# A preln graph network with a spectral layer, on one core: the setup of the Sturm sweeps re-divided between VectorE, ScalarE and GpSimd, and a block of ones written by another engine

## The chip, the cores and the metric

The program runs on one core of a Trainium2 chip. The time is the device time of one execution in microseconds (us); lower is better. TensorE (PE) does matrix products, VectorE (DVE), ScalarE (ACT) and GpSimd (POOL) work element by element on 128 partitions, SyncE (SP) issues the transfers. Each engine takes its own instructions in order; between engines, and between an instruction and an earlier one of the same engine whose result it reads, there are semaphores.

## What is computed

```python
h = jnp.maximum(_layernorm(x, axis=-1), 0.0)            # x: 32 x 256 x 128
x = x + _L0_gnn_ref(h, adj, W1, b1, W2, b2)
h = jnp.maximum(_layernorm(x, axis=-1), 0.0)
x = x + _L1_gnn_ref(h, adj, Wg0, bg0, Wg1, bg1, Wih, Whh, bih, bhh)

def _L0_gnn_ref(features, A, W1, b1, W2, b2):
    deg = jnp.sum(A, axis=0) + jnp.sum(A, axis=1) - jnp.diagonal(A)
    d_inv_sqrt = jnp.where(deg > 0, jax.lax.rsqrt(deg), 0.0)
    L_norm = d_inv_sqrt[:, None] * (jnp.diag(deg) - A) * d_inv_sqrt[None, :]
    _, U = jnp.linalg.eigh(L_norm)                       # 256 x 256
    agg = jnp.einsum('mn,bnd->bmd', U.T, features)
    out = jax.nn.relu(agg @ W1 + b1) @ W2 + b2
    return jnp.einsum('nm,bmd->bnd', U, out)
```

`_L1_gnn_ref` is two graph layers followed by four small LSTMs over windows of 1 to 4 rows. The change lies wholly in the eigenvectors of the 256 x 256 matrix.

## The kernel before

The 256 x 256 matrices lie as two blocks of 128 rows side by side on 128 partitions. The program goes through these stages.

First the start: GpSimd fills the constants (`ident`, `below`, `ones`, the zeroed NG, RC and V, `sgn` with ones, the index rows `tau_row` and `tau_col`, L263 to L297), VectorE and TensorE build the normalised Laplacian A with one square root on ScalarE (`sq`, L446) in the middle. ScalarE copies the transposed adjacency `adjT` first (L443).

Then the reduction to tridiagonal form: 255 steps k, one reflector each (VectorE L999 to L1081), every step a chain over VectorE, TensorE, ScalarE and GpSimd. It leaves the off-diagonal elements in NG[:, k, 0], scale factors in RC[:, k, 0:2], inner products in `sh` (ScalarE, L492), and the reflectors in V (GpSimd, L340).

Then the setup of the sweeps (VectorE, L1083 to L1119): the diagonal `dbc` = sh * RC squared, the negated squares `ne2` of the off-diagonal, its absolute values `off`, the Gershgorin bounds (greatest of `gh`, least of `gl`, in bnd[:, 0:2]), their span and its reciprocal bnd[:, 7:8], the first grid point bnd[:, 3:4], and `dbh`, `neh`, `e2mid`, the scaled halves of both diagonals, top half on partitions 0 to 63 and the mirrored bottom half on 64 to 127. `link(ins)` makes the next VectorE instruction wait for ins; `mark(ins)` only counts it. Beside this ScalarE takes the root `sc` of RC (L497), and GpSimd scales V by it to `Vh` (L351, two products), and then adds the gate biases `gate_b` (L368).

Then three sweeps (L1132 on) that count sign changes of a three-term recurrence at 64, 128 and 64 points: VectorE four chained instructions a step (L1165 to L1177), ScalarE the signs into `sgn` (L533), VectorE their changes `chg` (L1127), TensorE the counts (L774). In between, products for the accumulated reflectors are slipped in, with `Vh` as the first input (L647). `sgn` must hold ones in its first column block before the first `changes`. Then come the eigenvectors by a twisted factorisation, some filler products of TensorE ahead of the signs (L820, L823, the latter after the norms z_norm of L1361), U, the layers and the LSTMs.

The order of work on each engine is the order in which it is written.

## Time and profile before

| | |
|---|---|
| median of 3 runs | 1576.59 us (1576.54 to 1576.85) |
| the profiled execution's own time | 1576.68 us |
| its span, first to last instruction | 1574.9 us |
| busy: DVE / PE / ACT / POOL | 1252.9 / 1226.0 / 650.1 / 359.5 us |
| chain that ended last: DVE / PE / issue / ACT | 56 / 32 / 9 / 2 % |
| before the first reflector | 0 to about 18.3 us |
| reduction | to about 761.3 us |
| setup of the sweeps | 761.48 to 771.20 us |
| three sweeps | to about 1034 us |

Times in the trace are us from the span's start, and the profiled execution has some 1.8 us around its span. A row of a timeline is start, length, engine, line, operation, output <- inputs, shapes and count; behind it in brackets how long the engine stood idle before and what it waited for. The time from one start to the next says what an instruction costs its engine; two unchained instructions overlap by a little. Engine names with q are an engine's sequencer.

### The profile page before, as it was taken

How to read it: one execution, taken by the hardware profiler on the slowest of the kernel's cores; microseconds unless marked ns; L12 is line 12 of the kernel's file. 1: busy time of each engine (PE TensorE's matmuls, PEld its weight loads, DVE VectorE, ACT ScalarE, POOL GpSimd, SP SyncE). 2: the span in 40 equal slices, each digit the busy share in tenths (PEclk: the TensorE clock that was granted, in tenths of full speed). 3: DMA queues.
4: the chain of work that ended last, by engine and by line, in shares of the span. 5: the costliest groups of instructions: out<-in, count | busy, mean ns of one | idle time of the engine just before them, and what ended most of it. 6: DMA issues, size and time to landing. Idle time of an engine off the chain costs nothing.

```text
span 1574.9 us, 25121 instructions
## 1 busy us (share of the span) xinstructions
PE 1226.0 (78%) x5747; PEld 1006.4 (64%) x5747; DVE 1252.9 (80%) x6155; ACT 650.1 (41%) x2370; POOL 359.5 (23%) x1884
## 2 busy tenths in 40 slices
PE   6888889999976667777354454374999999999998
PEld 4666677777765555555243333262778789999997
DVE  7999999988888888888999999997682255555555
ACT  2333333443443444322121222250234587968676
POOL 5233323333345555555200000002000001010100
PEclk9999999999999999999967776787999999999999
DMA  7000000000000000000000000000000000001012
GB/s 174 2 1 1 1 1 1 1 1 2 1 1 1 1 1 1 1 1 1 1 0 1 1 0 1 0 1 0 1 1 1 0 1 1 1 1 28 1 28 55
DMA packets 23403, 12.63 MB, mean 8 GB/s; under 512 B 5075, under 2 KB 22230, under 8 KB 23254
## 3 DMA queue, kind: packets, MB, share of 16 engines
q1 hardware_dynamic: 23254, 11.03, 2.9%
q8 instruction: 46, 0.75, 0.2%
q14 instruction: 103, 0.84, 0.2%
HBM read 6.83 MB, written 4.19 MB: 7 GB/s over the span
## 4 chain that ended last, share of the span: by engine, by line
DVE 56%; PE 32%; issue 9%; ACT 2%; DVEq 1%; POOL 0%; POOLq 0%
PE bank L842 8%; DVE A L1081 5%; PE bank L844 5%; PE bank L851 4%; DVE RC L1169 4%; DVE O L1177 3%; DVE junk L1014 3%; DVE zc L1075 3%; DVE wk L1065 3%; DVE pa L1165 3%; DVE pc L1038 3%; DVE O L1173 3%; PE pair L842 2%; DVE gqn L1052 2%; DVE A L1071 2%
## 5 line engine op out<-in xcount | busy, mean ns | idle before, releaser
L490 ACT ACTIVATE ncp<-pc,RC 128x2 f32<-128x2 f32 (+1 forms) x254 | 74.9, 295 | 305.7 <-DVE RC L1041 305.7
L699 PE MATMUL bank<-O,y 128*128 128x2 f32 x510 | 142.3, 349 | 65.3 <-DVE y L1014 59.9
L629 ACT ACTIVATE H<-bank,gate_b 128x128 f32<-128x128 f32 (+2 forms) x468 | 167.4, 467 | 50.8 <-PE bank L844 37.8
L684 PE MATMUL bank<-ident,O 128*128 128x128 f32 x382 | 148.2, 457 | 51.4 <-DVE O L1058 38.1
L699 PEld LDWEIGHTS bank<-O,y 128*128 128x128 f32 x510 | 127.8, 311 | 77.7 <-issue 71.9
L684 PEld LDWEIGHTS bank<-ident,O 128*128 128x128 f32 x382 | 60.1, 197 | 139.4 <-DVE O L1058 139.4
L707 PE MATMUL pair<-ident,pc 128*128 128x128 f32 x381 | 145.2, 450 | 4.4 <-DVE pc L1038 1.1
L842 PE MATMUL bank<-O,WlT 128*128 128x128 f32 (+1 forms) x672 | 144.9, 326 | 4.6 <-DVE O L1445 2.8
L774 PE MATMUL bank<-chg,fold 128*128 128x512 bf16 x64 | 29.9, 594 | 139.2 <-DVE chg L1127 139.2
L319 POOL TENSOR_TENSOR ym<-y,below 128x2 f32<-128x2 f32 (+1 forms) x254 | 49.6, 195 | 349.9 <-DVE y L1024 249.9
L1071 DVE SCALAR_TENSOR_TENSOR A<-pair,cx,A 128x254 f32<-128x254 f32 (+63 forms) x380 | 121.3, 319 | 0.4 <-issue 0.2
L842 PEld LDWEIGHTS bank<-O,WlT 128*128 128x128 f32 x672 | 110.6, 190 | 16.6 <-ACT H L629 8.4
L533 ACT ACTIVATE sgn<-O 128x1024 bf16<-128x1024 f32 (+1 forms) x24 | 32.2, 1341 | 203.4 <-DVE O L1177 203.4
L1081 DVE SCALAR_TENSOR_TENSOR A<-bank,zc,A 128x254 f32<-128x254 f32 (+63 forms) x380 | 111.7, 321 | 4.5
L1470 DVE TENSOR_TENSOR H<-H 128x128 f32<-128x128 f32 (+2 forms) x96 | 33.4, 348 | 91.7 <-ACT H L629 91.7
L774 PEld LDWEIGHTS bank<-chg,fold 128*128 128x128 bf16 x64 | 5.7, 120 | 151.1 <-DVE chg L1127 121.9
L434 POOL COPY Wl<-O 128x344 f32<-128x344 f32 (+1 forms) x24 | 16.9, 753 | 373.0 <-DVE O L1450 373.0
L486 ACT ACTIVATE root<-bank 128x1 f32<-128x1 f32 x255 | 43.7, 171 | 133.6 <-PE bank L690 87.6
L844 PE MATMUL bank<-H,WlT 128*128 128x128 f32 (+1 forms) x480 | 98.2, 286 | 0.0
L695 PE MATMUL pair<-O,A 128*128 128x1 f32 x254 | 74.5, 362 | 24.6 <-DVE A L1081 21.3
L1014 DVE CUSTOM_DVE_ANT_0 junk<-A,bank 128x255 f32<-128x255 f32 (+63 forms) x382 | 89.8, 260 | 0.0
L695 PEld LDWEIGHTS pair<-O,A 128*128 128x128 f32 x254 | 63.7, 311 | 35.4 <-DVE A L1081 32.6
(444 smaller groups left out, 3444.6 us busy)
## 6 DMA issues: line engine op xcount, KB each, us to landing
X<-in_x SPq DMA_DIRECT2D x2, 2048.0 KB, 13.1
out<-X SPq DMA_DIRECT2D x32, 128.0 KB, 1.9
adj_sb<-in_adj SPq DMA_DIRECT2D x1, 256.0 KB, 3.0
W1s<-in_L_gnn_W SPq DMA_DIRECT2D x1, 64.0 KB, 11.1
W2s<-in_L_gnn_W SPq DMA_DIRECT2D x1, 64.0 KB, 4.1
Wg0s<-in_L_gnn_Wg SPq DMA_DIRECT2D x1, 64.0 KB, 3.9
Wg1s<-in_L_gnn_Wg SPq DMA_DIRECT2D x1, 64.0 KB, 3.7
Wl<-in_L_gnn_Wih SPq DMA_DIRECT2D x1, 0.5 KB, 6.9
```

The costliest lines, as they stand in the source:

```text
L490: a(ncp[:, bs], pc[:, bs], ACT.Identity, scale=RC[:, k, 1:2]).then_inc(S["ncp_ready"], 1)
L629: ins = a(gates[:, q, i, 0:n], gate_at(p, q, i), fn, bias=gate_b[:, p - 1, i:i + 1])
L684: ins = nc.tensor.transpose(xb[:, b * P:(b + 1) * P], R[:, b, k, 0:1].to_broadcast([P, P]), idf)
L695: mm(y01, A[:, 1, 0:P], R[:, 1, k, 0:1], start=True, stop=True).then_inc(S["y01_ready"], 1)
L699: ins = mm(sb_[:, 0:2], y[:, 1:2].to_broadcast([P, P]), R[:, 1, k, :], start=True, stop=(k >= P - 1))
L707: nc.tensor.transpose(prow[:, b * P:(b + 1) * P], pc[:, b:b + 1].to_broadcast([P, P]), idf).then_inc(S["prow1_ready" if b else "prow0_read ...
L842: last = mm(gate_at(p, q, i), WlT[:, 0, p - 1, i, :], window(c, p, t, part), start=True, stop=(t == 0))
L844: last = mm(gate_at(p, q, i), WlT[:, 1, p - 1, i, :], hst_at(p, q, n), start=False, stop=True)
L851: last = mm(bank[dst][:, a_ * N:(a_ + 1) * N], H[:, b, 2 * c + a_, :], M[:, b, :], start=(b == 0), stop=(b == 1))
L1014: v.tensor_tensor_reduce(out=junk2[:, b, c0:e], in0=A[:, b, c0:e], in1=xb[:, c0:e], scale=1.0, scalar=0.0, op0=ALU.mult, op1=ALU.add, accu ...
L1071: stt(out=A[:, b, c0 + 1:e], in0=prow[:, c0 + 1:e], scalar=cx[:, b:b + 1], in1=A[:, b, c0 + 1:e], op0=ALU.mult, op1=ALU.add).then_inc(S["a ...
L1081: stt(out=A[:, b, c0 + 1:e], in0=xb[:, c0 + 1:e], scalar=zc[:, b:b + 1], in1=A[:, b, c0 + 1:e], op0=ALU.mult, op1=ALU.add).then_inc(S["upd ...
```

## The change

The block of ones `sgn` (4352 columns in bf16) is no longer written by GpSimd's memset but by a ScalarE copy of a broadcast one, ahead of the copies of `adjT`; the counts of the semaphore `consts` go down by one everywhere. The two squares go to ScalarE, between its last `sh` and the root `sc`. The bounds are made by two VectorE instructions that each combine and take a maximum over the row (the least is the negated greatest of off-sum minus dbc), on one sum `gl` of neighbouring off-values. The copies into `dbh` and `neh` are laid between the one-column steps, and fewer instructions are chained. GpSimd's `Vh` waits for the bounds.

```diff
+            sgn_ones set_ready bounds_ready pre_ready lo_ready uv_ready cut_pre q_ready cut_ab cut_rec cut_g pick_ready cut_wh z_norm z_root z_signed zt_ps zt_cp u_ps u_cp
...
-            for t, val in ((NG, 0.0), (RC, -1.0), (V, 0.0), (sgn, 1.0)):
+            for t, val in ((NG, 0.0), (RC, -1.0), (V, 0.0)):
...
                 act, me = S["wy_act"], S["wy_pool"]
                 if i == 0:
                     pool.wait_ge(act, 1)
+                    pool.wait_ge(S["bounds_ready"], 1)
                     pool.wait_ge(S["v_ready"], K)
                     for b in range(NB):
                         ins = g.tensor_tensor(Vh[:, b], V[:, b], sc[:], ALU.mult)
...
         @block.scalar
         def _(act):
             a = nc.scalar.activation
+            act.wait_ge(S["consts"], 2)
+            a(sgn[:].rearrange("p j c w -> p (j c w)"), ones[:, 0:1].to_broadcast([P, 2 * (CH + 1) * PTS]), ACT.Copy).then_inc(S["sgn_ones"], 1)
             act.wait_ge(S["adjT_rdy"], 1)
             for j in range(NB):
                 a(adjT[:, j].rearrange("p (r b i) -> p b i r", r=2, b=NB), bank[6][:, j * N:(j + 1) * N].rearrange("p (b i r) -> p b i r", b=NB, r=2),
...
                     squares(k + 1)
                 norm1(k)
             act.wait_ge(S["c_ready"], K)
+            a(junk2[:, 0], RC[:, :, 0], ACT.Square).then_inc(S["set_ready"], 1)
+            a(ne2[:, 1:N + 1], NG[:, :, 0], ACT.Square).then_inc(S["set_ready"], 1)
             a(sc[:], RC[:, :, 1], ACT.Sqrt, scale=-1.0).then_inc(S["wy_act"], 1)
 
             def evac(dst, src, scale=1.0):
...
             dve.wait_ge(S["s_hist"], K)
             dve.wait_ge(S["d0_ready"], 1)
             pbs, rnb2 = NG[:, :, 0], junk2[:, 0]
-            v.tensor_copy(dbc[:, 0:1], bank[2][:, 0:1])
-            tt(rnb2, RC[:, :, 0], RC[:, :, 0], ALU.mult)
-            stt(out=ne2[:, 1:N + 1], in0=pbs, scalar=-1.0, in1=pbs, op0=ALU.mult, op1=ALU.mult)
             v.memset(ne2[:, 0:1], 0.0)
+            mark(v.tensor_copy(dbc[:, 0:1], bank[2][:, 0:1]))
             link(stt(out=off[:], in0=pbs, scalar=-1.0, in1=pbs, op0=ALU.mult, op1=ALU.max))
+            mark(v.tensor_copy(gl[:, 0:1], off[:, 0:1]))
+            mark(tt(gl[:, 1:N], off[:, 1:N], off[:, 0:N - 1], ALU.add))
+            dve.wait_ge(S["set_ready"], 1)
             link(tt(dbc[:, 1:N], sh[:, 0:K], rnb2[:, 0:K], ALU.mult))
-            link(ts(ne2[:, 1:N], ne2[:, 1:N], -E2_MIN, None, ALU.min))
-            link(tt(gh[:], dbc[:], off[:], ALU.add))
-            link(tt(gl[:], dbc[:], off[:], ALU.subtract))
-            link(tt(gh[:, 1:N], gh[:, 1:N], off[:, 0:N - 1], ALU.add))
-            link(tt(gl[:, 1:N], gl[:, 1:N], off[:, 0:N - 1], ALU.subtract))
-            link(v.tensor_reduce(bnd[:, 0:1], gh[:], AX.X, ALU.max))
-            link(v.tensor_reduce(bnd[:, 1:2], gl[:], AX.X, ALU.min))
-            link(tt(bnd[:, 2:3], bnd[:, 0:1], bnd[:, 1:2], ALU.subtract))
-            link(ts(bnd[:, 2:3], bnd[:, 2:3], 1e-6, None, ALU.max))
-
-            link(ts(bnd[:, 2:3], bnd[:, 2:3], 1.0 / SPAN, None, ALU.mult))
-            link(v.reciprocal(bnd[:, 7:8], bnd[:, 2:3]))
-            link(ts(bnd[:, 3:4], bnd[:, 1:2], bnd[:, 7:8], -0.005 * SPAN, ALU.mult, ALU.add))
+            v.tensor_tensor_reduce(out=gh[:], in0=dbc[:], in1=gl[:], scale=1.0, scalar=-3.0e38, op0=ALU.add, op1=ALU.max, accum_out=bnd[:, 0:1])
+            (v.tensor_tensor_reduce(out=junk2[:, 1], in0=gl[:], in1=dbc[:], scale=1.0, scalar=-3.0e38, op0=ALU.subtract, op1=ALU.max, accum_out=bnd[:, 5:6]).then_inc(S["bounds_ready"], 1))
+            v.tensor_copy(dbh[0:ROWS], dbc[0:ROWS, 0:STEPS])
+            dve.wait_ge(S["bounds_ready"], 1)
+            ts(bnd[:, 1:2], bnd[:, 5:6], -1.0, None, ALU.mult)
+            mark(tt(bnd[:, 2:3], bnd[:, 0:1], bnd[:, 5:6], ALU.add))
+            dve.wait_ge(S["set_ready"], 2)
+            ts(ne2[:, 1:N], ne2[:, 1:N], -1.0, -E2_MIN, ALU.mult, ALU.min).then_inc(S["dve_link"], 1)
+            n_link[0] += 1
+            dve.wait_ge(S["dve_link"], n_link[0] - 1)
+            mark(ts(bnd[:, 2:3], bnd[:, 2:3], 1e-6, 1.0 / SPAN, ALU.max, ALU.mult))
+            v.tensor_copy(dbh[ROWS:P], dbc[ROWS:P, N - 1:N - 1 - STEPS:-1])
+            dve.wait_ge(S["dve_link"], n_link[0])
+            mark(v.reciprocal(bnd[:, 7:8], bnd[:, 2:3]))
+            v.tensor_copy(neh[0:ROWS], ne2[0:ROWS, 0:STEPS])
+            mark(v.tensor_copy(neh[ROWS:P], ne2[ROWS:P, N:N - STEPS:-1]))
+            dve.wait_ge(S["dve_link"], n_link[0] - 1)
+            mark(ts(bnd[:, 3:4], bnd[:, 1:2], bnd[:, 7:8], -0.005 * SPAN, ALU.mult, ALU.add))
+            dve.wait_ge(S["dve_link"], n_link[0] - 1)
+            ts(dbh[:], dbh[:], bnd[:, 7:8], None, ALU.mult)
+            ts(neh[:], neh[:], bnd[:, 7:8], bnd[:, 7:8], ALU.mult, ALU.mult)
+            ts(e2mid[:], ne2[:, STEPS:STEPS + 1], bnd[:, 7:8], bnd[:, 7:8], ALU.mult, ALU.mult)
             tt(bnd[:, 4:5], bnd[:, 7:8], bnd[:, 7:8], ALU.mult)
             ts(bnd[:, 6:7], bnd[:, 7:8], -1.0, None, ALU.mult)
             step = 1.01 * SPAN / (ROWS * WIDTH[0])
...
             link(stt(out=bnd[:, 5:6], in0=bnd[:, 1:2], scalar=-1.0, in1=bnd[:, 0:1], op0=ALU.mult, op1=ALU.max))
             ts(bnd[:, 5:6], bnd[:, 5:6], bnd[:, 7:8], 8 * 2.0 ** -24, ALU.mult, ALU.mult).then_inc(S["pre_ready"], 1)
 
-            v.tensor_copy(dbh[0:ROWS], dbc[0:ROWS, 0:STEPS])
-            v.tensor_copy(dbh[ROWS:P], dbc[ROWS:P, N - 1:N - 1 - STEPS:-1])
-            v.tensor_copy(neh[0:ROWS], ne2[0:ROWS, 0:STEPS])
-            link(v.tensor_copy(neh[ROWS:P], ne2[ROWS:P, N:N - STEPS:-1]))
-            link(ts(dbh[:], dbh[:], bnd[:, 7:8], None, ALU.mult))
-            link(ts(neh[:], neh[:], bnd[:, 7:8], bnd[:, 7:8], ALU.mult, ALU.mult))
-            link(ts(e2mid[:], ne2[:, STEPS:STEPS + 1], bnd[:, 7:8], bnd[:, 7:8], ALU.mult, ALU.mult))
             def changes(n, w):
+                if n == 0:
+                    dve.wait_ge(S["sgn_ones"], 1)
                 dve.wait_ge(S["sgn_ready"], n + 1)
                 if n % 2 == 0 and n:
                     dve.wait_ge(S["sgn_carry"], n // 2)
```

VectorE at the setup, before, from the last reflector's end on; the names are those of the paragraph on the setup, `junk` holds the squares of RC.

```order
L1087 COPY dbc<-bank 128x1 [waits d0_ready,s_hist,c_ready]
L1088 TENSOR_TENSOR junk<-RC 128x256
L1089 SCALAR_TENSOR_TENSOR ne<-NG 128x256
L1090 MEMSET ne 128x1
L1091 SCALAR_TENSOR_TENSOR off<-NG 128x256
L1092 TENSOR_TENSOR dbc<-sh,junk 128x255 [waits dve_link]
L1093 TENSOR_SCALAR ne<-ne 128x255 [waits dve_link]
L1094 TENSOR_TENSOR gh<-dbc,off 128x256 [waits dve_link]
L1095 TENSOR_TENSOR gl<-dbc,off 128x256 [waits dve_link]
L1096 TENSOR_TENSOR gh<-gh,off 128x255 [waits dve_link]
L1097 TENSOR_TENSOR gl<-gl,off 128x255 [waits dve_link]
L1098 TENSOR_REDUCE bnd<-gh 128x1 [waits dve_link]
```

The same place now. ISA is a VectorE instruction that also accumulates, with a second row for writing the accumulator to `bnd`.

```order
L1092 MEMSET ne 128x1 [waits d0_ready,s_hist,c_ready]
L1093 COPY dbc<-bank 128x1
L1094 SCALAR_TENSOR_TENSOR off<-NG 128x256
L1095 COPY gl<-off 128x1 [waits dve_link]
L1096 TENSOR_TENSOR gl<-off 128x255
L1098 TENSOR_TENSOR dbc<-sh,junk 128x255 [waits set_ready]
L1099 ISA gh,bnd<-dbc,gl 128x256 [waits dve_link]
L1099 ISA bnd 128x1
L1100 ISA junk,bnd<-gl,dbc 128x256
L1100 ISA bnd 128x1
L1101 COPY dbh<-dbc 64x128
L1103 TENSOR_SCALAR bnd<-bnd 128x1 [waits bounds_ready]
```

Two squares are gone from VectorE, one sum stands for four, both reductions are folded into the ISA rows, and a copy of `dbh` stands ahead of the first wait for the bounds.

GpSimd among the constants, before:

```order
L276 MEMSET V 128x512
L276 MEMSET sgn 128x4352
L277 MEMSET eps_col 128x1
L278 IOTA fine 128x32
L280 IOTA junk 128x512
L284 IOTA grid 64x64 [waits consts]
L286 IOTA tau_col 64x4 [waits consts]
L284 IOTA grid 64x64 [waits consts]
```

and now:

```order
L276 MEMSET V 128x512
L277 MEMSET eps_col 128x1
L278 IOTA fine 128x32
L280 IOTA junk 128x512
L284 IOTA grid 64x64 [waits consts]
L286 IOTA tau_col 64x4 [waits consts]
L284 IOTA grid 64x64 [waits consts]
```

The memset of `sgn` is gone, and what stood behind it follows on V.

GpSimd at the end of the reduction, before:

```order
L338 TENSOR_TENSOR vt<-ident,NG 128x1 [waits v_ready,pb_ready,x_ready]
L340 TENSOR_TENSOR V<-O,vt 128x1 [waits vt_ready]
L351 TENSOR_TENSOR Vh<-V,sc 128x256 [waits v_ready,wy_act]
L351 TENSOR_TENSOR Vh<-V,sc 128x256
L368 TENSOR_TENSOR gate_b<-gate_in 128x16 [waits b_in]
L355 AFFINE_SELECT Pm<-Gs 128x512 [waits wy_act]
```

and now:

```order
L338 TENSOR_TENSOR vt<-ident,NG 128x1 [waits v_ready,pb_ready,x_ready]
L340 TENSOR_TENSOR V<-O,vt 128x1 [waits vt_ready]
L352 TENSOR_TENSOR Vh<-V,sc 128x256 [waits v_ready,bounds_ready,wy_act]
L352 TENSOR_TENSOR Vh<-V,sc 128x256
L369 TENSOR_TENSOR gate_b<-gate_in 128x16 [waits b_in]
L356 AFFINE_SELECT Pm<-Gs 128x512 [waits wy_act]
```

The rows are the same; the first product waits for one semaphore more, and the rest stands behind it.

## Rows read from the trace of the kernel before

**Rows 1.** Timeline of the start: start, length, engine, line, operation, operands, count.

```profile
4.69 3.73 POOL L276 MEMSET sgn<- 128x4352 bf16 x1
...
5.03 1.07 ACT L443 ACTIVATE adjT<-pair 128x256 f32<-128x256 f32 x2 [2.96 <-PE pair L662]
...
6.12 1.28 ACT L446 ACT_TABLE_LOAD   x1
...
6.80 1.68 DVE L973 TENSOR_SCALAR pos<-deg 128x2 f32<-128x2 f32 x1
...
9.44 0.20 ACT L446 ACTIVATE sq<-deg 128x2 f32<-128x2 f32 x1 [2.03 <-DVE deg L975]
...
10.07 0.68 DVE L980 TENSOR_SCALAR tmp<-ident,dinv 128x256 f32<-128x256 f32 x2
...
12.11 1.50 POOL L294 TENSOR_SCALAR tau_row<-junk 128x512 bf16<-128x512 f32 x1
...
13.37 0.52 DVE L984 TENSOR_SCALAR tmp<-ident 128x512 f32<-128x512 f32 x1
```

**Rows 2.** Timeline of the setup of the sweeps, up to the first sweep instruction.

```profile
761.48 0.16 DVE L1087 COPY dbc<-bank 128x1 f32<-128x1 f32 x1 [0.23 <-ACT sh L492]
761.56 0.41 DVE L1088 TENSOR_TENSOR junk<-RC 128x256 f32<-128x256 f32 x1
761.79 1.63 POOL L351 TENSOR_TENSOR Vh<-V,sc 128x256 f32<-128x256 f32 x2 [0.40 <-ACT sc L497]
761.89 0.95 DVE L1089 SCALAR_TENSOR_TENSOR ne<-NG 128x256 f32<-128x256 f32 x1
762.77 0.93 DVE L1091 SCALAR_TENSOR_TENSOR off<-NG 128x256 f32<-128x256 f32 x1
...
763.38 0.40 POOL L368 TENSOR_TENSOR gate_b<-gate_in 128x16 f32<-128x16 f32 x1
...
764.52 0.43 DVE L1094 TENSOR_TENSOR gh<-dbc,off 128x256 f32<-128x256 f32 x1
764.98 0.42 DVE L1095 TENSOR_TENSOR gl<-dbc,off 128x256 f32<-128x256 f32 x1
...
768.43 0.15 DVE L1110 SCALAR_TENSOR_TENSOR bnd<-bnd 128x1 f32<-128x1 f32 x1
...
768.74 0.21 DVE L1113 COPY dbh<-dbc 64x128 f32<-64x128 f32 x1
768.96 0.22 DVE L1114 COPY dbh<-dbc 64x128 f32<-64x128 f32 x1
...
770.01 0.35 DVE L1118 TENSOR_SCALAR neh<-neh,bnd 128x128 f32<-128x128 f32 x1
...
770.71 0.25 DVE L1135 TENSOR_SCALAR lam<-grid,bnd 128x64 f32<-128x64 f32 x1
771.20 0.28 DVE L1165 SCALAR_TENSOR_TENSOR pa<-lam,dbh,O 128x64 f32<-128x64 f32 x1 [0.24 <-DVE lam L1135]
```

**Rows 3.** Timeline of the first sweep, where a GpSimd product lies beside VectorE.

```profile
796.51 1.30 POOL L359 TENSOR_TENSOR RT<-ident,PmT 128x512 f32<-128x512 f32 x1 [7.18 <-ACT PmT L500]
796.61 1.28 DVE L1165 SCALAR_TENSOR_TENSOR pa<-lam,dbh,O 128x64 f32<-128x64 f32 x1
```

**Rows 4.** One line's instructions: shortest/median/longest ns, first and last start, forms.

```profile
L533 ACT ACTIVATE sgn<-O x24: 1057/1057/1911, 778.7 to 1027.2; 128x1024 bf16<-128x1024 f32 x16, 128x2048 bf16<-128x2048 f32 x8
```

**Rows 5.** Timeline, VectorE: a product with an accumulated sum.

```profile
1089.54 0.42 DVE L1361 CUSTOM_DVE_ANT_0 junk<-adj_sb 128x256 f32<-128x256 f32 x1
```

**Rows 6.** Timeline of TensorE: its first product with Vh.

```profile
783.77 3.02 PE L647 MATMUL bank<-Vh 128*128 128x256 f32 x8
```

**Rows 7.** Busy by stretch, PE, PEld, DVE, ACT, POOL, then granted clock, DMA, GB/s.

```profile
1084.00:1085.00 1.00, 1.00 (x2) 0.36 (x2) 1.00 (x4) 0.00 (x0) 0.90 (x2) 0.50 0.06 16
```

**Rows 8.** One line's instructions: shortest/median/longest ns, the first filler products.

```profile
L820 PE MATMUL bank<-WlT,ident x10: 592/592/1190, 1083.6 to 1088.9; 128*128 128x512 f32 x10
```

**Rows 9.** Timeline of TensorE: the filler products behind z_norm.

```profile
1090.38 2.84 PE L823 MATMUL bank<-WlT,ident 128*128 128x512 f32 x6 [0.87 <-DVE ssq L1361]
```

15 lines of the change are left out of this document (7 added, 8 removed).

## The prediction

> **What bounds the kernel now.** I read the chain of waits first. It runs through the places that this change touches and nowhere near a DMA: the start up to the first reflector, and a stretch of almost ten microseconds between the reduction and the first sweep in which VectorE works alone. The profiled execution took 1576.68 us against a median of 1576.59, so a sum made in it is moved down by 0.09. The reader needs two timelines.
>
> The start [rows 1]: VectorE's tiny TENSOR_SCALAR on deg (L973, two columns) takes 1.68 us, because it lies beside GpSimd's 3.73 us memset of sgn. It ends only when that memset has ended (4.69 + 3.73 = 8.42). So ScalarE's root sq, ready since its table load ended at 7.40, starts at 9.44, and all that follows hangs on it.
>
> The setup [rows 2]: from L1087 at 761.48 to the first step of the sweep at 771.20 are 9.72 us, nearly all on VectorE and nearly all chained by link. In it, GpSimd's two products Vh (1.63 us together) make two VectorE instructions of 256 columns, L1089 and L1091, take 0.95 and 0.93 us, where L1088 and L1094 of the same width take 0.41 and 0.43. The same is seen in the first sweep [rows 3]: a 64-column instruction lasts 1.28 us beside a GpSimd product of 1.30 us that it began 0.10 us after. So for these kinds of operands one engine stands still until the other's instruction is over; 512 columns hold it about 1.3 us, and 256 columns about 0.66.
>
> **The start, part by part.** The memset leaves GpSimd, so what is behind it moves up 3.7 us. ScalarE instead writes 4352 columns before the two adjT copies. Its row for bf16 from f32 [rows 4] gives 1057 ns for 1024 columns and 1911 for 2048: 0.834 ns a column and 0.20 us fixed, so 3.83 us. Its first table load should end at about 2.1 (the second takes 1.28 us; the first is taken to be as long and to begin at 0.8, an estimate). The write then ends at 5.9; the adjT copies begin about 5.75 in place of 5.03, end at 6.8 (1.07 us), and the table load behind them ends at 8.1 in place of 7.40 [rows 1]. VectorE's three little instructions no longer meet the memset; they meet short copies of GpSimd and should be through by 7.3 to 7.9. So ScalarE's own chain becomes what sq waits for: sq at 8.1, which is 1.3 us early.
>
> That is not kept. L980 follows sq by 0.63 us and would start at 8.75. GpSimd's tau_row, at 12.11 with 1.50 us, moves up to about 8.2 to 8.4 and runs to 9.7 to 9.9. That it holds a TENSOR_SCALAR is in the trace: L984 begins at 13.37 inside it, and ends 0.28 after tau_row's end at 13.61 [rows 1]. So the pair L980 ends at about 10.0 to 10.4, against 10.75 now: 0.35 to 0.75 us gained. L984, no longer beside tau_row, gives another 0.1. I take **0.6 us**; the bounds are 0.1 (the write on ScalarE is slower, or L980 waits for tau_col and fold too) and 1.4 (tau_row does not hold it).
>
> **The setup without GpSimd.** VectorE's new list, start to start [rows 2]: memset and one-column copy 0.16 (L1087 to L1088 is 0.08); off, chained, 0.46 (L1094 to L1095); one-column copy 0.08; gl, which nothing is chained to, 0.33 (L1088 to L1089); dbc, chained, 0.46; the two products with an accumulated maximum. The nearest row for these is the accumulated sum L1361 of 256 columns with 0.42 us [rows 5], and with 0.07 of overlap 0.35 each, 0.70. Together 2.19 us, and both bounds are there at 763.67. A maximum is not in the trace; below this it can hardly go, as 256 columns cost 0.33 at the least in any unchained row, and above it I allow 0.3 us each.
>
> Then, with the copies laid between the one-column steps: copy of dbh until the bounds can be read, 0.13, and two steps of 0.08, 0.29; ne2 0.20; the scaled span, 0.16, since the copy behind it begins at another partition (L1113 to L1114 is 0.22, the whole length of a copy, so such a copy waits for the one before); copy 0.23; reciprocal 0.09; two copies 0.23 and 0.25. That is 1.45. The bnd step 0.13, dbh 0.20 and neh 0.27 (L1135 with 0.25 and L1118 with 0.35, each less 0.08 of overlap, and 0.03 for the wider tile), e2mid 0.20: 0.80. Four last steps: 0.15, and 0.31 as from L1110 to L1113. lam to the first pa, 0.49. The whole is 2.19 + 1.45 + 0.80 + 0.46 + 0.49 = 5.39 us against 9.72: 4.33 us less. What goes is the squares (to ScalarE, which does them right behind the last sh, each 0.42 us by the two lengths in [rows 4], and has them at about 761.7 and 761.9, while VectorE wants them at 762.5 and 764.0), three of the four sums and two reductions, for which one sum and the two accumulating products stand, and most of the chained pauses.
>
> **The wait that is added.** GpSimd's Vh now waits for bounds_ready, about 763.75, and with it gate_b and the rest of GpSimd's queue. TensorE does not mind: its first product with Vh is at 783.77 [rows 6], and Vh would be ready at about 765.3. VectorE does. At 763.8 its next instructions are the two bnd steps and ne2, with two SBUF inputs or of the TENSOR_SCALAR kind, just those that stood still above. Two products of 0.66 us and a small gate_b pass, one VectorE instruction between each: VectorE reaches the scaled span about 1.3 us late, at 765.4 instead of 764.16. So the stall of L1089 and L1091 (1.0 us) is not removed but moved, and it is now 1.3. The setup gains 4.33 - 1.3 = **3.0 us**; first sweep step near 768.2.
>
> Here a page bears on the number. The reported lengths of GpSimd, 1.63 for the pair and 0.40 for gate_b [rows 2], would make the stall 2.0 us. The Trainium skill (Perfetto Trace Analysis, GPSIMD Engine Instruction) says that such spans are unreliable and that instructions are to be timed by start-to-start spacing; the two Vh products end at 763.42 with one VectorE stream of 0.27 us between them, and by that they are 0.68 each. By the reported spans the setup would gain 2.3, by spacing 3.0.
>
> A second page speaks of who is held at all. The Trainium skill (SBUF — State Buffer, Who interferes with whom) says that the pair of ports shared by VectorE and GpSimd is locked for a whole instruction, and that an instruction with two SBUF inputs contends with GpSimd's reads only, one in a two-port mode with anything of GpSimd. L973 beside a memset, and L1165 beside a product, agree with it.
>
> **Sum.** 0.6 + 3.0 = 3.6 us: 1576.68 - 3.6 - 0.09 = **1573.0 us**. The sweeps, the layers and the recurrent part are the same instructions, and only begin earlier.
>
> **Rivals.**
> 1. *No stall in the setup*: the one-column steps pass beside Vh, or VectorE gets ahead. For it: no one-column SBUF step is seen beside a long GpSimd product before. Against: ne2 has 255 columns, and L1091's kind did stand still. Time 1576.59 - 0.6 - 4.3 = 1571.7.
> 2. *tau_row does not hold L980*, if GpSimd's list is later or sooner than I place it. The start gains 1.4: 1576.59 - 1.4 - 3.0 = 1572.2.
> 3. *The stalls are as long as the reported spans, on both places*: 0.4 at the start and 2.3 in the setup, or the accumulated maxima cost 0.3 more each: 1573.9. For it: L973 shows how a tiny instruction can be held through several. Against: the spacing of Vh.
> 4. *Slower*: TensorE's clock. The filler products ahead of the signs, five and then three, begin at granted clock 0.50, the level of 1.2 GHz [rows 7]; each is two records, which go from 1190 to 592 ns when it rises to 2.4 GHz [rows 8]. The last three lie on the chain, 2.84 us for six records, with 0.87 us idle ahead [rows 9]. If the shifted program found the clock low through these six (3.6 us more) and through the two full products behind them (3.0 us more each at most, as much as L647 takes in [rows 6]), it would lose up to 9.6 us and stand at 1582. It costs nothing up to a rise 1.7 us later (0.87 us at half speed), and outweighs the gain of 3.6 from a rise 9 us later. Against: three runs lie within 0.31 us.
>
> **Chances.** Forecast 0.58, rival 1 0.09, rival 2 0.08, rival 3 0.20, rival 4 and other mishaps 0.05. The range from 1571.6 to 1574.2 takes in rivals 1 to 3 and leaves out the fourth and the outer bounds. 0.2% is 3.15 us, about what a measurement can tell from no change, and the line is at 1573.44, near to my number. The forecast lies under it in four of five, rivals 1 and 2 wholly, rival 3 in one of five: 0.69 faster, 0.27 the same, 0.04 slower.
>
> **What would show it.** At the start: sgn on ScalarE of about 3.8 us, L973's counterpart under 0.4 us, sq near 8.1, the pair of tmp at 10.0 to 10.4. In the setup: the maxima at 0.42 us, bnd steps and ne2 of 0.7 to 0.9 us beside Vh, and 6.7 us from the one-column copy to the first pa. Wrong if ScalarE loads a table between the squares and the root, if the bnd steps are short while Vh runs, or if the first pa comes after 769.

## The result and the profile after

The kernel after the change takes 1571.18 us (median of 6 runs, 1570.37 to 1572.52), the kernel before 1576.95 us beside it (6 runs, 1576.54 to 1577.31). The ratio is 0.9966, with a 95% interval of 0.9955 to 0.9976: faster by more than 0.2%, by about 5.8 us where 3.6 were forecast, and 0.4 us below the range of 1571.6 to 1574.2. The profiled execution took 1570.37 us, with a span of 1568.6 us. It is the fastest of the six and lies 0.8 us under their median, where the profile of before lies 0.3 us under its own, so 0.5 us of the distance between the two profiles is spread and not the change.

The page after: the span, the busy times, and the shares of the chain that ended last.

```profile
span 1568.6 us, 25122 instructions
...
PE 1224.6 (78%) x5747; PEld 1005.1 (64%) x5747; DVE 1247.5 (80%) x6153; ACT 657.3 (42%) x2373; POOL 352.9 (22%) x1883
...
DVE 55%; PE 33%; issue 9%; ACT 2%; DVEq 1%; POOL 0%; POOLq 0%
```

VectorE has 5.4 us less work (it had 1252.9). The chain has kept its shares (56 / 32 / 9 / 2 before), so nothing new bounds the kernel. The gain must be looked for by stages. Four marks divide the span: the first `half` (the end of the start), the one-column copy into `dbc` (the end of the reduction), the first `pa`, and the first norm behind the sweeps (z_norm). Each is the start of that VectorE instruction in the timeline.

| us | start | reduction | setup | sweeps | rest |
|---|---|---|---|---|---|
| before | 19.3 | 742.2 | 9.7 | 318.3 | 485.3 |
| before, a second profile | 19.3 | 743.1 | 9.7 | 318.3 | 485.5 |
| after | 18.4 | 741.2 | 6.1 | 317.4 | 485.5 |
| after, a second profile | 18.4 | 742.3 | 6.1 | 318.5 | 485.4 |
| after, a third | 18.4 | 741.0 | 6.1 | 319.0 | 485.2 |

Start and setup repeat to 0.1 us. The reduction and the sweeps differ by up to 1.3 and 1.6 us between executions of one kernel, so of them a single pair of profiles proves nothing.

The start of after, which answers to [rows 1]; columns as there.

```profile
2.08 3.83 ACT L443 ACTIVATE sgn<-ones 128x4352 bf16<-128x4352 f32 x1
...
6.87 1.28 ACT L449 ACT_TABLE_LOAD   x1
...
8.17 0.20 ACT L449 ACTIVATE sq<-deg 128x2 f32<-128x2 f32 x1
8.29 1.50 POOL L294 TENSOR_SCALAR tau_row<-junk 128x512 bf16<-128x512 f32 x1
...
8.61 0.30 DVE L983 TENSOR_TENSOR dinv<-dinv,pos 128x2 f32<-128x2 f32 x1
8.94 0.99 DVE L985 TENSOR_SCALAR tmp<-ident,dinv 128x256 f32<-128x256 f32 x2
...
9.99 2.07 PE L675 MATMUL bank<-tmp,ones 128*128 128x256 f32 x4 [3.56 <-DVE tmp L985]
...
12.55 0.43 DVE L989 TENSOR_SCALAR tmp<-ident 128x512 f32<-128x512 f32 x1
...
18.38 0.16 DVE L1014 TENSOR_SCALAR half<-bank 128x1 f32<-128x1 f32 x1 [0.81 <-PE bank L689]
```

`sgn` on ScalarE is as forecast (2.08, 3.83 us), the root `sq` is at 8.17 instead of 9.44, and `tau_row` lies over the pair of `tmp`, as forecast. But the pair ends at 9.93, under the forecast of 10.0 to 10.4, and the scaled identity (L989, once L984 with 0.52) lasts 0.43. The first `half` comes 0.89 us earlier. The line of the pair, with the shortest, the middle and the longest of the two in ns:

```profile
L985 DVE TENSOR_SCALAR tmp<-ident,dinv x2: 354/538/723, 8.9 to 9.2; 128x256 f32<-128x256 f32 x2
```

The first one passes beside `tau_row` in 0.35 us. The second lasts 0.72 us instead: it is held, and ends 0.14 behind the reported end of `tau_row` (8.29 + 1.50 = 9.79).

The setup of after, which answers to [rows 2].

```profile
759.37 0.42 ACT L500 ACTIVATE junk<-RC 128x256 f32<-128x256 f32 x1
...
759.60 0.16 DVE L1093 COPY dbc<-bank 128x1 f32<-128x1 f32 x1
...
761.33 0.42 DVE L1100 CUSTOM_DVE_ANT_0 junk<-gl,dbc 128x256 f32<-128x256 f32 x1
...
761.81 0.14 DVE L1103 TENSOR_SCALAR bnd<-bnd 128x1 f32<-128x1 f32 x1
761.88 0.14 DVE L1104 TENSOR_TENSOR bnd<-bnd 128x1 f32<-128x1 f32 x1
761.89 1.45 POOL L352 TENSOR_TENSOR Vh<-V,sc 128x256 f32<-128x256 f32 x2 [2.42 <-DVE bnd L1100]
761.94 0.82 DVE L1106 TENSOR_SCALAR ne<-ne 128x255 f32<-128x255 f32 x1
762.68 0.14 DVE L1109 TENSOR_SCALAR bnd<-bnd 128x1 f32<-128x1 f32 x1
762.85 0.57 DVE L1110 COPY dbh<-dbc 64x128 f32<-64x128 f32 x1
763.30 0.21 POOL L369 TENSOR_TENSOR gate_b<-gate_in 128x16 f32<-128x16 f32 x1
...
765.68 0.28 DVE L1175 SCALAR_TENSOR_TENSOR pa<-lam,dbh,O 128x64 f32<-128x64 f32 x1 [0.24 <-DVE lam L1145]
```

From the one-column copy to the first `pa` are 6.08 us (759.60 to 765.68), against 9.72. The squares are on ScalarE, the maxima cost 0.42 us each, like the accumulated sum of [rows 5], and 0.08 for the read of the result. The reader is to see in what order things come at 761.8: both bnd steps (L1103, L1104) are issued before Vh (761.89) and last 0.14. Two VectorE instructions are held, ne2 (0.82) and the copy into `dbh` (0.57). The one-column TENSOR_SCALAR between them, at 762.68 and so in the middle of Vh (its second product is reported from 762.57 to 763.34), lasts 0.14 and is not.

### The profile page after: what moved, and what is told of

Read it like the earlier page. It is cut to its first block, busy times and chain, and to the rows that moved or that the text cites. A ratio compares the mean times of both kernels' runs of the same rounds, so it can differ in the third digit from the quotient of the medians.

```text
span 1568.6 us, 25122 instructions
## 1 busy us (share of the span) xinstructions
PE 1224.6 (78%) x5747; PEld 1005.1 (64%) x5747; DVE 1247.5 (80%) x6153; ACT 657.3 (42%) x2373; POOL 352.9 (22%) x1883
## 4 chain that ended last, share of the span: by engine, by line
DVE 55%; PE 33%; issue 9%; ACT 2%; DVEq 1%; POOL 0%; POOLq 0%
PE bank L847 8%; DVE A L1086 5%; PE bank L849 5%; PE bank L856 4%; DVE RC L1179 4%; DVE O L1187 4%; DVE junk L1019 3%; DVE zc L1080 3%; DVE pc L1043 3%; DVE wk L1070 3%; DVE pa L1175 3%; PE pair L847 3%; DVE O L1183 3%; DVE gqn L1057 2%; DVE A L1076 2%
```

## The experiments

Two questions stood open: how the 5.8 us divide, and what of it is the reduction, whose instructions nobody touched. Times are medians, with the ratio to the kernel before in runs of the same chip and its 95% interval. Five groups of kernels ran, each beside its own runs of before.

### The two kernels again, and each half alone

`before_again` and `after_again` are the two kernels unchanged. `start_only` is before with the change of `sgn` alone:

```diff
-            for t, val in ((NG, 0.0), (RC, -1.0), (V, 0.0), (sgn, 1.0)):
+            for t, val in ((NG, 0.0), (RC, -1.0), (V, 0.0)):
...
+            act.wait_ge(S["consts"], 2)
+            a(sgn[:].rearrange("p j c w -> p (j c w)"), ones[:, 0:1].to_broadcast([P, 2 * (CH + 1) * PTS]), ACT.Copy).then_inc(S["sgn_ones"], 1)
```

`setup_only` is the other half: after with `sgn` still a memset of GpSimd, all else of the change in.

> The kernel before, unchanged, under a second name. Theory A (the two places account for the change, and the rest of the difference between the two profiles, 1.8 us spread over the reduction and what follows the setup, is spread between executions): ratio to before 1.000 within 0.001, and the time from the first reflector's half (L1009) to the one-column copy (L1087) differs from the first profile's 742.2 us by some tenths of a us up to 1 us. Theory B (the change itself makes the reduction and the rest faster): that time repeats within 0.2 us.

> The changed kernel, unchanged, under a second name. Theory A: 4.5 us below before (0.90 at the start, 3.64 in the setup), so ratio 0.9971. Theory B: 5.8 us or more below, ratio 0.9963 or less, and the reduction again about 1 us shorter than in the kernel before.

> The kernel before with the ones of sgn written by ScalarE and nothing else. Theory A: first reflector 0.9 us earlier, as in the profile of the changed kernel, the setup unchanged at 9.72 us; 0.9 us below before, ratio 0.9994. Theory B, that the change at the start also shortens the reduction: 1.9 us or more below. The sum of my prediction had 0.6 us here.

> The changed kernel with sgn written by GpSimd's memset as before, so only the setup is new. Theory A: first reflector where it was before (root at 9.44), setup 6.1 us instead of 9.7, 3.6 us below before, ratio 0.9977. Theory B, a faster rest behind the setup: 4.5 us or more below. The sum of my prediction had 3.0 us here.

| | median us | ratio | start | reduction | setup |
|---|---|---|---|---|---|
| before_again | 1577.24 | 1.0001 [0.9992, 1.0010] | 19.3 | 743.1 | 9.7 |
| after_again | 1571.88 | 0.9969 [0.9958, 0.9981] | 18.4 | 742.3 | 6.1 |
| start_only | 1575.55 | 0.9992 [0.9983, 1.0001] | 18.4 | 742.1 | 9.7 |
| setup_only | 1573.56 | 0.9978 [0.9970, 0.9987] | 19.2 | 742.9 | 6.1 |

The kernel before stood at 1577.18. `setup_only` gains 3.62 us, which is its setup (9.72 - 6.08 = 3.64) and nothing else. `start_only` gains 1.63, of which its start explains 0.9. Together they are 5.25, and `after_again` gains 5.30, between the 4.5 of theory A and the 5.8 of theory B: by the medians the halves add up. The interval of `start_only` reaches 1.0001, so its median can't carry the rest alone; the steps below do. The surplus of 0.7 to 0.8 us belongs to the half that moves `sgn`, but lies behind the first `half`.

To find it I took the distance from each step's first `half` to the next one's. Most of the 254 distances scatter a little. But in steps 3, 19, 35, 51, 67, 83, 99 and 115, sixteen apart, each takes one of two values, 0.05 to 0.18 us from each other: step 83 has 3.37 us in before and 3.26 in after. These eight sum to 28.29 to 28.33 us in `before`, `before_again` and `setup_only`, and to 27.50 to 27.56 in `after`, `after_again` and `start_only`. (Sums of starts read to 0.01 us.) That is 0.8 us, and what was sought. (Behind step 127, steps 187, 188 and 244 differ too, two by -0.1 and one by +0.17, and cancel.)

### What holds VectorE in the setup

`no_bounds_wait` takes out the added wait, so that Vh starts when `sc` is there:

```diff
                     pool.wait_ge(act, 1)
-                    pool.wait_ge(S["bounds_ready"], 1)
                     pool.wait_ge(S["v_ready"], K)
```

`vh_one_column2` keeps the wait and shrinks what waits to one column. It leaves out nearly all of the scaling of V, so its time shows an unhampered setup:

```diff
+            g.memset(Vh[:], 0.0)
...
-                        ins = g.tensor_tensor(Vh[:, b], V[:, b], sc[:], ALU.mult)
+                        ins = g.tensor_tensor(Vh[:, b, 0:1], V[:, b, 0:1], sc[:, 0:1], ALU.mult)
```

> The changed kernel without GpSimd's wait for the bounds: Vh starts when ScalarE's root sc is there, about 0.9 us into the setup. Theory A (a GpSimd product of 256 columns holds each VectorE instruction of two wide SBUF inputs, or of the two-port kind with more than one column, for about 0.66 us wherever it lies): now the dbc product and the first accumulated maximum are held, the setup is about 6.3 us instead of 6.1, 0.2 us slower than the changed kernel, ratio to before 0.9972. Rival (the place does not matter or the wait costs): the setup is 5.2 us, 0.9 us faster than the changed kernel.

> The changed kernel with both products Vh cut to one column each (the rest of Vh is set to zero in the constants, so this leaves out nearly all of the scaling and the eigenvectors aren't computed). Theory A: nothing holds ne2 (0.29 us instead of 0.82) and the second copy of dbh (0.22 instead of 0.57); the setup is 5.2 us instead of 6.1, my sum of unheld durations having been 5.4. Rival (the two are long for another reason, such as the order of partitions): the setup stays at 6.1 us.

`no_bounds_wait`: 1571.32 us, ratio 0.9967 [0.9955, 0.9980], setup 6.1 us. `vh_one_column2`: 1571.34, 0.9967 [0.9954, 0.9979], setup 5.2 us. (Before: 1576.64, for these two and the next two.) The timeline of the setup in `no_bounds_wait`:

```profile
760.75 1.86 POOL L351 TENSOR_TENSOR Vh<-V,sc 128x256 f32<-128x256 f32 x2 [1.05 <-ACT sc L501]
761.20 0.83 DVE L1098 CUSTOM_DVE_ANT_0 gh<-dbc,gl 128x256 f32<-128x256 f32 x1
...
761.96 0.93 DVE L1099 CUSTOM_DVE_ANT_0 junk<-gl,dbc 128x256 f32<-128x256 f32 x1
...
763.10 0.27 DVE L1105 TENSOR_SCALAR ne<-ne 128x255 f32<-128x255 f32 x1
```

Without the wait Vh meets the two maxima instead, which last 0.83 and 0.93 us instead of 0.42, and ne2 is free (0.27). The expectation had named the product into `dbc` and the first maximum; `dbc` starts together with Vh and takes its usual 0.42. The stall is moved, not removed: the setup is 6.13 us against 6.08, so the added wait is worth 0.05 us. The same place in `vh_one_column2`:

```profile
763.17 0.38 POOL L353 TENSOR_TENSOR Vh<-V,sc 128x1 f32<-128x1 f32 x2 [2.42 <-DVE bnd L1101]
763.22 0.28 DVE L1107 TENSOR_SCALAR ne<-ne 128x255 f32<-128x255 f32 x1
763.42 0.14 DVE L1110 TENSOR_SCALAR bnd<-bnd 128x1 f32<-128x1 f32 x1
...
763.59 0.23 DVE L1111 COPY dbh<-dbc 64x128 f32<-64x128 f32 x1
```

Here nothing is held, ne2 takes 0.28 instead of 0.82 and the copy 0.23 instead of 0.57. The two differences are 0.54 + 0.34 = 0.88 us, the same as 6.08 - 5.20 between the setups. So the stall of Vh in after is 0.9 us, and the list without it is 5.2 us.

Yet the kernel with the shorter setup is no faster than after (it gains 5.30 us on its own runs of before, `after_again` on its own as much). Its eight steps sum to 28.37: it has the long ones again, with the change of `sgn` in. It has one more memset of GpSimd in its start, and so had before. That was the first hint.

### Is it the number of GpSimd instructions ahead of the loop?

`after_plus_one` is after with one memset more, a repetition, and `before_minus_one` is before with one memset fewer: of the five memsets of `begin_sweep`, two rows three apart and of one value are written by one.

```diff
+            g.memset(eps_col[:], EPS)
```

```diff
-            begin_sweep()
+            for row, rows, val, d in ((14, 1, 0.0, 1), (15, 1, 1.0, 1), (30, 4, 0.0, 3), (31, 2, 1.0, 1)):
+                ins = g.memset(poly[:, row:row + rows:d], val)
+            ins.then_inc(S["ring_ready"], 1)
```

> The changed kernel with one more GpSimd instruction ahead of the reduction, a memset of the one-column eps_col that repeats its value. Theory C (in every 16th step of the reduction one of GpSimd's instructions comes 0.29 us late, which one depends on how many instructions stand ahead in its stream, and taking the memset of sgn away moved the lateness from ym, for which VectorE waits, to one that nobody waits for): steps 3, 19, 51, 67, 83, 99 and 115 are long again, as in the kernel before (3.37 us for step 83 instead of 3.27), step 244 short again, and the reduction is 0.8 us longer; 0.8 us slower than the changed kernel, ratio to before 0.9974. Rival (ScalarE's writing of sgn, or an earlier start, shortens the steps): step 83 stays at 3.27.

> The kernel before with the first begin_sweep's two zero rows set by one memset instead of two, so one GpSimd instruction fewer ahead of the reduction, nothing else. Theory C: ym is no longer late in every 16th step, step 83 takes 3.27 us instead of 3.37, the reduction is 0.8 us shorter, start and setup as before; ratio 0.9995. Rival: the steps stay as in the kernel before.

`after_plus_one`: 1572.84 us, 0.9972 [0.9961, 0.9983]. `before_minus_one`: 1576.45, 0.9996 [0.9987, 1.0004], with before at 1577.27. Step 83 in four kernels, GpSimd's `ym` and VectorE's `tm`, which reads it. Before:

```profile
309.63 0.20 POOL L319 TENSOR_TENSOR ym<-y,below 128x2 f32<-128x2 f32 x1 [2.15 <-DVE y L1024]
...
309.86 0.22 DVE L1047 SCALAR_TENSOR_TENSOR tm<-ym,RC,tmp 128x2 f32<-128x2 f32 x1 [0.21 <-POOL ym L319]
```

After:

```profile
307.84 0.20 POOL L319 TENSOR_TENSOR ym<-y,below 128x2 f32<-128x2 f32 x1 [1.87 <-DVE y L1029]
...
308.25 0.24 DVE L1052 SCALAR_TENSOR_TENSOR tm<-ym,RC,tmp 128x2 f32<-128x2 f32 x1
```

After plus one memset:

```profile
308.98 0.20 POOL L320 TENSOR_TENSOR ym<-y,below 128x2 f32<-128x2 f32 x1 [2.15 <-DVE y L1030]
...
309.20 0.22 DVE L1053 SCALAR_TENSOR_TENSOR tm<-ym,RC,tmp 128x2 f32<-128x2 f32 x1 [0.20 <-POOL ym L320]
```

Before minus one memset:

```profile
309.06 0.20 POOL L321 TENSOR_TENSOR ym<-y,below 128x2 f32<-128x2 f32 x1 [1.87 <-DVE y L1026]
```

The bracket behind `ym` is GpSimd's idle time: 2.15 us in the first and third, 1.87 in the other two, as in the steps around. In the first and third GpSimd starts `ym` 0.28 us later for no reason that the row names (its input is VectorE's `y` in all four), and `tm` waits for it (0.21 and 0.20 us idle, released by `ym`). All the steps agree: in before and after plus one `ym` starts 0.43 to 0.50 us behind the end of `y` in the eight steps 3, 19, ..., 115 and 0.14 to 0.15 in the rest of the first 127, in after and before minus one 0.14 to 0.15 in every one. The sum of the eight steps is 28.33 us in `after_plus_one` and 27.56 in `before_minus_one`. One GpSimd instruction put in or taken out ahead of the loop decides, and it was another one each time: the memset of `sgn`, of `eps_col`, of `Vh`, of a row of `poly`. It isn't the time at which the loop begins: `tau_row_last`, below, begins it at 19.2 us, as `setup_only` does, and has the short steps; `after_plus_one` at 18.4 has the long ones. The medians agree in size (each beside its own before, `after_plus_one` gains 4.43 us where `after_again` gains 5.30, and `before_minus_one` gains 0.82), but their intervals alone would not carry it.

### Why one instruction is late: blocks of the instruction stream

The view of DMA shows a kind of transfer that no line of the kernel issues. Two us of before with step 83's `ym` in them (309 to 311), the DMA's busy tenths in 40 slices, and the queue with its packets:

```profile
DMA  0000000000000000000000000600000000000000
...
q14 instruction: 1, 0.01, 1.5%
```

One packet, in the 26th slice, at 310.25 to 310.30 us: 8192 bytes of instructions. The 2 us ahead (306 to 308, step 82) have none. The same queue has a packet in each of the eight steps 3, 19, ..., 115, about 2 us behind the first `half` of the step, in before and in after alike. The packet of step 83 begins 0.6 us behind the late `ym` (309.63), so it isn't what `ym` waits for; it only marks the step. This suggested a theory: GpSimd's instructions come in blocks, the step across a block's edge costs it 0.28 us, and VectorE feels it only where the edge lies between the waits of `ym` and `ym` itself. The count ahead of the loop sets where the edges lie. How many places of the stream a step takes can be counted in before: six GpSimd instructions, and two waits that have a record of their own, one of them (L318, once in each of the first 127 steps) just ahead of `ym`:

```profile
L318 POOLq EVENT_SEMAPHORE  x127: 17/17/17, 20.3 to 448.5; - x127
```

That makes eight. From this record to the start of `ym` are 0.40 to 0.46 us in the eight steps and 0.11 in every other one: the delay lies just between these two. Three more kernels are after with 2, 8 and 9 more memsets, each of another column:

```diff
             begin_sweep()
+            for i in range(9):
+                g.memset(Vh[:, 0, i:i + 1], 0.0)
```

> Two memsets of one column of Vh are put ahead of the reduction on GpSimd, so two instructions more stand in its queue than in the kernel after. Theory of blocks: the profile has instruction transfers of 8192 bytes on one queue; one falls 1.95 us after the first half of step 83 in the kernel before, and none in step 82. GpSimd has six instructions a step and two of them wait for two semaphores, so I take eight places a step in its instruction stream, and 128 places a block: a block's edge comes back at the same place every 16 steps. Its crossing costs GpSimd about 0.28 us, and VectorE sees it only where the edge lies directly ahead of ym, which VectorE waits for, behind ym's waits. With two more the edge lies ahead of ym's own waits, in its idle time of 1.87 us: the eight steps 3, 19, ..., 115 sum to 27.5 us, as in after. Rival, more instructions always mean the long steps: 28.3. Rival, every second count gives the long steps: 27.5 too, so this run alone does not decide against it.

> Eight memsets of one column of Vh ahead of the reduction on GpSimd. Theory of blocks: the edge lies just one step earlier than in the kernel after, behind ym in steps 2, 18, ..., 114, where nobody waits for it: no long steps, the eight steps 3, 19, ..., 115 sum to 27.5 us and the eight ahead of them (2, 18, ..., 114) to 27.7, both as in after. Rival, more instructions mean the long steps: 28.3 and 27.7. The first half comes up to 0.4 us later if GpSimd's start still matters.

> Nine memsets of one column of Vh ahead of the reduction on GpSimd. Theory of blocks: this is after plus one moved by a whole step, so the long steps are back, but one step earlier: the steps 2, 18, ..., 114 sum to 28.5 us instead of 27.7, and 3, 19, ..., 115 stay at 27.5. Rival, every second count gives the long steps at their old place: 27.7 and 28.3. Rival, the late instruction has nothing to do with the stream's blocks: neither moves by one step.

| more than after | steps 2, 18, ..., 114 | steps 3, 19, ..., 115 | median us | ratio |
|---|---|---|---|---|
| 0 | 27.66 | 27.50 | 1571.18 | 0.9966 [0.9955, 0.9976] |
| 1 | 27.73 | 28.33 | 1572.84 | 0.9972 [0.9961, 0.9983] |
| 2 | 27.70 | 27.55 | 1571.88 | 0.9964 [0.9951, 0.9978] |
| 8 | 27.69 | 27.56 | 1571.27 | 0.9966 [0.9951, 0.9982] |
| 9 | **28.42** | 27.49 | 1572.71 | 0.9973 [0.9959, 0.9986] |

With nine more the long steps are back and lie one step earlier, as expected (28.5), and with two or eight they are gone. That more instructions always mean long steps, and that every second count does, are both out. The late `ym` of `after_plus_nine` in step 82, and the `tm` that waits for it:

```profile
305.62 0.20 POOL L321 TENSOR_TENSOR ym<-y,below 128x2 f32<-128x2 f32 x1 [2.17 <-DVE y L1031]
...
305.85 0.22 DVE L1054 SCALAR_TENSOR_TENSOR tm<-ym,RC,tmp 128x2 f32<-128x2 f32 x1 [0.20 <-POOL ym L321]
```

And the DMA of 305 to 307 us in the same kernel:

```profile
DMA  0000000000000000000000000000003000000000
...
q14 instruction: 1, 0.01, 1.0%
```

The transfer has moved with it, to 306.50 to 306.55; the windows of 304 to 306 and 308 to 310 have none. With eight and with nine more, the packets of steps 3, 19, ..., 115 stand in 2, 18, ..., 114, while others of the same queue (step 85, for one) stay where they were. After has its packet in step 83 like before, at 308.80. By the count its edge lies one place further on, behind `ym`, where GpSimd waits for RC anyway; that is worked out and not seen, for none of GpSimd's eight records comes late in these steps of after. That nine acts as one does, a step earlier, says again that eight places of GpSimd's stream make a step; 16 steps make 128 places, and 8192 bytes over 128 are 64 bytes each. The Trainium skill (Runtime: NRT & Kernel Launch, Instruction fetch mechanics) states that an engine's instructions are refilled in blocks of 16 KiB or 256 instructions, which is also 64 bytes each, and calls the cost of crossing an edge mostly hidden. The block's size differs here: the queue that moved with GpSimd's count has packets of 8192 bytes. In the traces the cost doesn't show with 0, 2 and 8 more, and is 0.28 us of GpSimd and some 0.1 us a step of VectorE with 1 and 9 more; other counts were not tried. What the 0.28 us consist of, no row shows.

### Can the start be had without the neighbours?

`tau_row_last` moves GpSimd's `tau_row` behind the memsets of `begin_sweep`; `both_moves` also moves the write of `sgn` behind the root on ScalarE. The edit of the first:

```diff
-            g.tensor_scalar(tau_row[:], junk2[:].rearrange("p b n -> p (b n)"), 0.5, None, ALU.mult).then_inc(S["consts"], 1)
             g.tensor_scalar(tau_col[:], tau_col[:], 0.5, None, ALU.mult).then_inc(S["consts"], 1)
-            pool.wait_ge(S["consts"], 23)
+            pool.wait_ge(S["consts"], 22)
...
+            g.tensor_scalar(tau_row[:], junk2[:].rearrange("p b n -> p (b n)"), 0.5, None, ALU.mult).then_inc(S["consts"], 1)
```

and in `both_moves` also the two lines of `sgn` stand behind the two of `sq`. `both_moves_again` is the same kernel a second time.

> The changed kernel with GpSimd's tau_row moved behind the memsets of begin_sweep. Theory A (tau_row holds the pair tmp at L985 until its end at 9.79): the pair takes 0.5 us instead of 0.99, or a few tenths more beside GpSimd's short fold and memsets, TensorE's broadcast starts at about 9.5 instead of 9.99, the first reflector 0.4 to 0.5 us earlier. Rival: the pair stays at 0.99 us beside whatever GpSimd does then.

> The changed kernel with tau_row behind begin_sweep's memsets and ScalarE's write of sgn behind the root sq instead of ahead of adjT. Theory A (sq waits for ScalarE's own chain of 3.83 us, adjT and the table load): adjT starts near 5.0, its table load ends near 7.4, sq starts near 7.4 instead of 8.17, the broadcast near 8.7 instead of 9.99, first reflector 1.2 us earlier; 1.2 us below the changed kernel, ratio to before 0.9962. Rival: sq is held by VectorE's three small instructions beside GpSimd, and starts after 7.8.

> The same as both_moves, for its time and its start a second time: first reflector 0.9 us earlier than in the changed kernel (17.5 against 18.4), the rest as in the changed kernel; 0.9 us below it, 5.4 + 0.9 = 6.3 us below before, ratio 0.9960.

`tau_row_last`: 1571.20 us, 0.9968 [0.9957, 0.9980]; `both_moves`: 1570.61, 0.9963 [0.9949, 0.9976]; again 1571.32, 0.9962 [0.9949, 0.9976]. The first `half` stood at 19.2 us in the first and 17.5 in the others, where 18.4 is after's. For `tau_row_last` the expectation failed: the start is 0.8 us longer than after's, not 0.4 to 0.5 shorter. Its median doesn't show that, as its six runs spread over 1.6 us; its timeline does, and says why:

```profile
8.59 0.54 POOL L296 TENSOR_SCALAR fold<-fold 128x128 bf16<-128x128 bf16 x1
...
8.92 1.79 DVE L985 TENSOR_SCALAR tmp<-ident,dinv 128x256 f32<-128x256 f32 x2
9.07 0.89 POOL L300 MEMSET O<- 128x128 f32 x5
9.93 1.52 POOL L304 TENSOR_SCALAR tau_row<-junk 128x512 bf16<-128x512 f32 x1
```

```profile
L985 DVE TENSOR_SCALAR tmp<-ident,dinv x2: 684/932/1181, 8.9 to 10.0; 128x256 f32<-128x256 f32 x2
```

With `tau_row` gone, the first of the pair lay beside the end of `fold` and five memsets, and took 1.18 us, to 0.14 behind the last memset's end at 9.96; the second then met `tau_row` after all, took 0.68, and was through at 10.71, long before `tau_row`'s end at 11.45. In after the first took 0.35. Here a run of short instructions held one VectorE instruction from beginning to end, and a long one let one through. In `both_moves` the root comes 0.86 us earlier, and the pair slips in ahead of the memsets:

```profile
7.31 0.20 ACT L447 ACTIVATE sq<-deg 128x2 f32<-128x2 f32 x1
7.42 3.81 ACT L449 ACTIVATE sgn<-ones 128x4352 bf16<-128x4352 f32 x1
...
7.75 0.56 DVE L983 TENSOR_TENSOR dinv<-dinv,pos 128x2 f32<-128x2 f32 x1
...
8.34 0.67 DVE L985 TENSOR_SCALAR tmp<-ident,dinv 128x256 f32<-128x256 f32 x2
...
9.11 0.89 POOL L300 MEMSET O<- 128x128 f32 x5
```

It is the start that gains: 0.9 us against after, of the 1.2 expected. The missing 0.3 is L983, 0.56 instead of 0.30 beside GpSimd's copy into R (its rows call the tile O). The median does not tell the two apart; the mark does.

`constants_behind_diag` goes on from there: GpSimd's last constants wait for the pair (diag_rdy), in the order tau_row, fold, the copy of R, tau_col. `memsets_behind_lap` is the same, with the memsets waiting for the Laplacian as well. `after_third` is after once more, on the same chip as the latter.

```diff
+            pool.wait_ge(S["diag_rdy"], 1)
+            g.tensor_scalar(tau_row[:], junk2[:].rearrange("p b n -> p (b n)"), 0.5, None, ALU.mult).then_inc(S["consts"], 1)
...
+            pool.wait_ge(S["lap_rdy"], 1)
```

(the second wait in `memsets_behind_lap` alone.)

> both_moves with GpSimd's constants that read or write wide tiles (tau_row, the halving of fold, R's second column, tau_col, the memsets) put behind VectorE's pair tmp, where VectorE waits 2.1 us for TensorE's broadcast. Theory A (each GpSimd instruction beside VectorE's dinv product and the pair holds them): dinv at 0.16 us instead of 0.56, the pair at 0.5 instead of 0.67, the first reflector 0.5 us earlier than in both_moves, 17.0. Rival: what GpSimd does later then holds VectorE's ts on ident or the products into A, and the 0.5 us are lost again. One wait more stands in GpSimd's stream; if waits count in it as memsets do, the every-16th-step lateness moves and the reduction changes by up to 0.8 us either way.

> constants_behind_diag with the five memsets of begin_sweep behind VectorE's last product into A, where VectorE waits 1.2 us for TensorE's transposes. Theory D (a run of memsets without a gap holds a VectorE instruction of the two-port kind until the last of them): the scaled ident takes 0.43 us or at most 0.7 beside tau_col, instead of 1.34, and the first reflector is 0.9 us earlier than in constants_behind_diag, 17.2 against 18.1; 1.2 us below the changed kernel, ratio to before 0.9959. Rival (tau_col or R's copy held it): it stays above 1 us.

> The changed kernel a third time, beside memsets_behind_lap: by stages 0.9 at the start, 0.8 in the reduction and 3.64 in the setup, 5.4 us below before, ratio 0.9966.

`constants_behind_diag`: 1571.88 us, 0.9967 [0.9954, 0.9979], first `half` at 18.1. The pair of `tmp` was through at 8.72, but the memsets had found the next TENSOR_SCALAR:

```profile
11.34 1.34 DVE L990 TENSOR_SCALAR tmp<-ident 128x512 f32<-128x512 f32 x1
...
11.52 0.89 POOL L302 MEMSET O<- 128x128 f32 x5
```

1.34 us instead of 0.43 take back what the pair had won: 18.1 and not the 17.0 expected, as its rival had it. With the memsets behind the Laplacian, beside TensorE's transposes, where VectorE has nothing to do:

```profile
11.34 0.51 DVE L991 TENSOR_SCALAR tmp<-ident 128x512 f32<-128x512 f32 x1
...
13.73 0.89 POOL L302 MEMSET O<- 128x128 f32 x5 [2.16 <-DVE A L994]
```

the same instruction takes 0.51 us, with `tau_col` beside it as before, so it was the memsets that held it. The first `half` is at 17.2. `memsets_behind_lap` takes 1569.56 us, 0.9958 [0.9945, 0.9970], with before at 1576.00 and `after_third` at 1570.99 (0.9969 [0.9956, 0.9981]). It gains 6.44, of which 2.0 at the start, 3.64 in the setup and 0.8 in the eight steps. It has the lowest ratio of all, 1.4 us under `after_third`; the two intervals overlap, but the mark at the first `half` (17.2 against 18.4) gives 1.2 of it.

## Why the prediction was wrong, by its steps

**What bounds the kernel** was right: the chain kept its shares, and both places that the chain of waits had named gave time. By the profile the gain is 0.89 (start) + 3.64 (setup) + 0.79 (eight steps, 28.29 - 27.50) = 5.32 us, against 5.30, 5.77 and 5.01 by the medians of three groups of runs; what is beyond is within the spread of the executions. The miss of the forecast by the profile is 1.7 us: 0.3 in the first term, 0.6 in the second and 0.8 in a third that was set to nothing. The range was left by 0.4 us, less than the medians of after differ from group to group (1570.99 to 1571.88), so that the time fell outside is in part chance; the three terms are not, for each is read from marks that repeat to 0.1 us.

**The start, 0.6 forecast, 0.89 measured.** The mechanism held at each point: the length of the write (3.83), the root at 8.1 (8.17), and `tau_row` over the pair. The size was off because I let the pair end 0.3 to 0.5 us behind `tau_row`; only its second instruction was held, and it ended 0.14 behind, at 9.93, so TensorE started its products at 9.99, 0.81 earlier than before (10.80). That a hold lasts to the reported end could not be read from L984 in [rows 1]: it began 0.24 us ahead of that end and was only 0.09 longer than the 0.43 it takes here. The rest is L989, 0.43 instead of 0.52, as put. The value lies within the bounds of 0.1 to 1.4.

**The setup, 3.0 forecast, 3.64 measured.** The unhampered list was 5.2 us (`vh_one_column2`) and not 5.39. The stall was 0.9 and not 1.3, and that is the mis-sized term. I let Vh meet three VectorE instructions, one between each of its parts, the bnd steps among them. But these were issued 0.08 and 0.01 us ahead of it, the one-column step inside it was not held at all, and gate_b, 0.21 us, held nothing that the rows show. Two instructions remained, 0.54 and 0.34 us. The second was held for less because it came 0.28 us after its product had begun (762.85 against 762.57). That ne2 would be held for 0.7 to 0.9 us (0.82) was right, that the bnd steps would be was wrong.

**"The same instructions, and only begin earlier": the step that failed.** I set the reduction to nothing because the diff does not touch it. But it takes one instruction out of GpSimd's queue ahead of the 255 steps, and that moves the edges of its instruction blocks off the place just ahead of `ym`, where VectorE waits. It was there to be seen in before: eight steps too long by 0.1 us, sixteen apart, each with an instruction transfer. With this term at 0.8 the forecast would have been 1572.2, and the range, moved as much, 1570.8 to 1573.4, would have held the result. (For the range alone the 0.6 us of the setup would have done it too.)

**The rivals.** (1) No stall in the setup: the stall was there, a third smaller. Its reason was half true, the one-column steps pass. Its 1571.7 is nearest to the result, but by a sum of other terms. (2) `tau_row` does not hold the pair: it did, 0.99 against 0.68 us. (3) Stalls as long as GpSimd's reported spans: Vh is reported with 1.45 us and gate_b with 0.21, and together they held VectorE 0.9. The Trainium skill (Perfetto Trace Analysis, GPSIMD Engine Instruction), by which such spans are not to be trusted, agrees with that, though most of the difference is that VectorE had not arrived yet. From start to start the two products are 0.68 us apart (761.89 to 762.57), the length that the forecast took for one. (4) The clock of TensorE: sweeps and rest are 317.4 to 319.0 and 485.2 to 485.5 us in after against 318.3 and 485.3 to 485.5 in before; nothing was lost. The ten first filler records were slower in after (a median of 1061 ns, where before has 592), but the six behind z_norm took 592 each. The rival's own sum is 1573.0 + 9.6 = 1582.6, not 1582.

**Who is held.** The Trainium skill (SBUF — State Buffer, Who interferes with whom) has the shared ports locked for a whole instruction. The two-input maxima beside Vh in `no_bounds_wait` (0.83 and 0.93 us) agree. Three rows go beyond it: the first of the pair in `tau_row_last` stood through several memsets and not through one instruction, and the first of the pair in after (0.35) and the second in `tau_row_last` (0.68) got through beside `tau_row`. The measurement decides here. Nor does a hold last to the reported end: the held instructions end 0.14 us (L985) behind that of `tau_row`, 0.15 (ne2) and 0.08 (the copy) behind those of the two products Vh, and 0.14 behind the last memset's, where unheld they take 0.35, 0.28, 0.23 and 0.35. If they run at their own speed once free, GpSimd let go 0.13 to 0.21 us ahead of its reported end (an estimate from these rows).

**The width of the range.** Its lower end was rival 1's number less 0.1, with nothing kept for work the diff leaves alone. Three terms were each too small on the same side, and the bounds of the start alone (up to 1.4) would have reached 1570.9 together with rival 1.

## What to carry to other kernels

A sum over the edited lines is not the whole price of an edit: an instruction more or less ahead of a long loop moves the edges of that engine's instruction blocks through every step behind it, so compare the loop step by step, and where single steps at a fixed distance differ, look for the instruction transfers in the DMA view. Where two engines hold each other, write down to the tenth of a microsecond what each of them issues around the moment of the wait, for here an instruction issued as little as 0.01 us ahead of the other was free. Moving a transfer of ports or a product out of one neighbour's way finds the next; the place to look for is one where the other engine has nothing to do, as behind the Laplacian here.

## What the runs showed of the hardware

- In before, GpSimd starts `ym` 0.28 us late in eight of the first 127 steps, sixteen apart, each with an 8192-byte instruction transfer; one instruction more or less ahead of the loop hides it or brings it out, for 0.8 us of the whole.
- Five GpSimd memsets in a row, 0.89 us together, stretched one VectorE TENSOR_SCALAR of 256 columns to 1.18 us and one of 512 columns to 1.34, where 0.35 and 0.43 are seen elsewhere.
- A one-column TENSOR_SCALAR of VectorE ran in 0.14 us in the middle of the GpSimd products that held one of 255 columns for 0.54 us and a copy of 128 columns for 0.34.
